# Five edits to a four-layer graph network kernel: zeros of the adjacency, entries of two layers, alternating PSUM banks in the edge loop

## The chip, the cores and the metric

The kernel is one program on one core of a Trainium2 chip. The metric is the device time of one execution in microseconds (us); lower is better. The program's queues are PE (matmul), ACT, DVE (vector), POOL (GpSimd) and SP, which only issues transfers.

## The reference

A graph of 3125 nodes with 64 features each and 103,125 edges (50,000 random pairs in both directions and a self loop for each node), sorted by destination; each edge has one of 16 types. Four layers run one after the other, each as `x = x + layer(relu(layernorm(x)))`:

- L0: two SAGE convolutions (`segment_sum(x[src], dst) @ Wl.T + bl + x @ Wr.T`) with a row normalisation between them.
- L1: relational sums; an edge of type r adds `h[src] @ weight[r]` to its destination.
- L2: three GAT attention convolutions, each with self loops added: `softmax` over the incoming edges of `leaky_relu(h[src] @ a_src + h[dst] @ a_dst)`, weighting `h[src]`.
- L3: two mean SAGE convolutions with batch norm and leaky ReLU.

## The kernel before

**Layout.** Nodes lie as 25 tiles (NT) of 125 partitions (P), so features are `[125, 25, 64]`; five chunks (NC) of five tiles (TC) are the unit of the pipelines. The adjacency `adj` holds the number of edges between each pair of nodes in FP16, 25 tiles of 125 x 3146 (39,325 FP32 words on each partition). It must be zero before it is built, and it serves L0, L2 and L3.

**Preparation (L165 to L258).** SP loads the edge tables, then features and matrices (L170 to L176); after the index work on DVE it stores `key_table` (L178). POOL fills the first half of `adj` with zeros (L188), ACT the second (L200), while DVE waits for nothing but its tables and runs a chain of index operations (L217 to L258). The block ends when all engines have, SP's waits for every load among them. Then comes a loop that builds `adj` by one-hot matmuls (L364).

**L1's entry (L398 to L719).** Before L1 the last five tiles of `adj` are stored in DRAM (`adj_saved`), since L1 uses their space for its buffers. A block does LayerNorm over all 25 tiles, `x_saved` is stored (L398), a second block splits the normalised features into FP16 high and low parts (`h_parts`, L644 to L653) and stores them as `h_table` in DRAM (L658, L659), and a third loads the relation weights (L695, L696, scaled at L703), makes an index row by a POOL `iota` (L708, cast at L719) and zeroes the sums `aggT`.

**L1's edge loop (L738 to L1030).** 34 turns (TURNS), each with six groups (`pos` 0 to 5) of 512 edges. Of these, POOL fetches four (`pos` 0, 1, 3, 4: buffers 0 to 3) with four indirect gathers each (L761) from `h_table`; each gather buffer is free again once PE's `z` of that position in the turn before is done. The other two (`pos` 2 and 5) are picked by PE: DVE makes 25 one-hot `select` rows of 1024 edges (L951, five buffers), and PE multiplies `h_parts` with them (`pick`, L896, two matmuls each) into PSUM banks 3 and 4. At the turn's end ACT copies banks 3 and 4 to `picked_T` (L812), PE turns the eight blocks (`turned`, L906) into banks 5 and 6, and ACT copies these to `pair_pick` (L817), which the next turn's `z` 2 and 5 read. `z` (L875) multiplies gathered rows with one-hots of destination and type (DVE L939, ACT L794 and L800), ACT copies `z` out of PSUM (L824), and `outputs` (L885) applies the 16 relation weights, in six parts over the next turn. DVE adds the 20-column windows to `aggT` (L963). PE's order in a turn is written out by hand:

```python
z(j, pos)
if pos == 0 and not static(j, 0):
    turned(j)
if not static(j, LAST):
    pick(j, lo, hi)
if not static(j, 0):
    outputs(j - 1, 1 - half, *PARTS[pos])
```

After the loop two turns' windows are added, each with its base loaded just before (`base_of`), the barriers pass and SP clears 23 semaphores.

**L2's entry (L1244 to L1342).** SP reloads `x_saved`, the vectors and the five tail tiles of `adj` (L1250 to L1253), each as one transfer of 125 rows; DVE waits for the features, adds L1's sums by chunk (L1270), does LayerNorm over all tiles (L1275 to L1285) and the attention vectors' columns of three layers (L1294, L1295); PE turns and projects chunk by chunk (L1579, L1587). POOL adds self loops to the first 20 tiles (L1473), sets constants (L1476, L1480), adds the self loops of the tail tiles as they land (L1485), and takes the maximum over partitions (L1488), on which DVE's next steps wait (L1316, then L1342). PE counts degrees (L1562) once all self loops are in. L2's first columns follow at L1342 on DVE.

Of the kernel before, what the change touches and what calls it, by code (L numbers as in the profile page):

```python
# [38 lines left out]
PICKED = {2: 0, 5: 1}  # L39
TAIL = 20  # L40
# [30 lines left out]
def gnn(nc, x_in, dst_groups, src_groups, src_tiles, dst_tiles, type_tiles, mats_in, vecs_in, rel_in, out):  # L71
    ctx = ExitStack()
    with ctx:
# [50 lines left out]
        node_key = sb("node_key", [P, NT], FP32, edge_scope)  # L124

# [12 lines left out]
        iota_h = sb("iota_h", [128, W * NT], FP16, build_scope)  # L138
# [20 lines left out]
        zero_cut = adj_words.shape[1] // 2  # L159
# [5 lines left out]
        with block as block:  # L165
            @block.sync
            def _(sp):
# [4 lines left out]
                sp.dma_start(ti[:, 2, :], type_tiles).then_inc(s_ti, 16)  # L172
                sp.dma_start(x_sb[:, :, :], x_in).then_inc(s_x, 16)
# [3 lines left out]
                sp.wait_ge(s_key, 1)  # L177
                sp.dma_start(key_table.rearrange("(k g) e -> g k e", g=128), key_i.bitcast(FP16)).then_inc(s_keys, 16)  # L178
                for s in (s_mats, s_mats2, s_vecs, s_x, s_keys):
                    sp.wait_ge(s, 16)  # L180

            @block.gpsimd
            def _(pool):
# [4 lines left out]
                pool.memset(adj_words[:, 0:zero_cut], 0.0).then_inc(s_zeroed, 1)  # L188
# [83 lines left out]
        with nc.Fori(0, passes):  # L272
            with nc.Block() as block:
                @block.vector
# [304 lines left out]
        with nc.Block() as block:  # L579
            @block.sync  # L580
            def _(sp):
                sp.dma_start(adj_saved, adj_tail).then_inc(s_spill, 16)
                for done in (s_sg, s_key, s_keys, s_nodes, s_dg, s_ti, s_x, s_mats, s_mats2, s_vecs, s_zeroed, s_zeroed2, s_iota,
                             s_ident, s_ident2, s_chain, s_diag, s_basebc, s_span, s_spanall):
                    sp.sem_clear(done)
# [47 lines left out]
        with ExitStack() as scope:  # L633
            h = sb("l1_h", [P, NT, D], FP32, scope)
            tmp = sb("l1_tmp", [P, NT, D], FP32, scope)

            layer_norm_relu("l1", h[:, :, :], tmp[:, :, :], dmas=[(x_saved, x_flat)])
            s_hs, s_table, s_hp, s_lp = (sem("l1_" + n) for n in ("h_scaled", "table_stored", "high_parts", "low_parts"))
            cut = 112
            rows = table.rearrange("(t p) d -> p t d", p=P)  # L640
            with nc.Block() as block:
                @block.vector
                def _(dve):
                    nc.vector.tensor_scalar(tmp[:, :, :], h[:, :, :], LO_SCALE, None, ALU.mult).then_inc(s_hs, 1)  # L644
                    dve.wait_ge(s_hp, 1)
                    dve.wait_ge(s_hs, 1)
                    nc.vector.scalar_tensor_tensor(h_parts[:, :, D:2 * D], h_parts[:, :, 0:D], -LO_SCALE, tmp[:, :, :],
                                                   ALU.mult, ALU.add).then_inc(s_lp, 1)
                    dve.wait_ge(s_lp, 1)

                @block.scalar
                def _(act):
                    act.activation(h_parts[:, :, 0:D], h[:, :, :], ACT.Copy).then_inc(s_hp, 1)  # L653

                @block.sync
                def _(sp):
                    sp.wait_ge(s_lp, 1)
                    sp.dma_start(rows[0:cut], h_parts[0:cut, :, :]).then_inc(s_table, 16)  # L658
                    sp.dma_start(rows[cut:P], h_parts[cut:P, :, :]).then_inc(s_table, 16)  # L659
                    sp.wait_ge(s_table, 32)  # L660
                    sp.wait_ge(s_spill, 16)

# [1074 lines left out]
```

## Time and profile before

| | |
|---|---|
| time, median of 3 | 2373.18 us (2372.23 to 2378.6) |
| the profiled execution | 2376.6 us, its span 2374.8 us |
| PE / DVE / ACT / POOL busy | 75% / 70% / 52% / 47% of the span |
| mean granted TensorE clock | 0.89 |
| preparation | 0 to 35.5 us |
| building `adj` | 35.5 to 375 us |
| L0 | 376.5 to 487.2 us |
| L1's entry | 487.7 to 516.5 us |
| L1's edge loop, its closing barriers with it | 516.5 to 1437.1 us |
| L2's entry, up to DVE L1342 | 1437.1 to 1489.4 us |
| L2 and L3 | to 2374.8 us |

The stages follow one another: a barrier stands between them. So what a stage saves at its end is saved in the whole, and what an engine saves inside a stage only counts if the stage's end moves. The profiled execution took 3.4 us more than the median, 0.14%.

### The profile page before, as it was taken

The numbers are of one execution on the slowest core, as the hardware profiler recorded it, in microseconds if no ns is written. First come the engines' busy times: TensorE is split into PE (matmuls) and PEld (weight loads), VectorE is DVE, ScalarE is ACT, GpSimd is POOL, SyncE is SP. The second block draws the span as 40 slices with busy tenths as digits, with TensorE's granted clock in tenths as the row PEclk, the third lists the DMA queues.
The fourth block names the chain that finished last, engine by engine and source line by source line (L and its number), as shares of the span: only waits on it lengthen the run. The fifth ranks groups of instructions, "written<-read, shape, count | busy, mean of one in ns | idle before, by whom it ended". The sixth has DMA issues, their size and how long they took to land. (4 is left out here: it accounts for less than half of the span.)

```text
span 2374.8 us, 34792 instructions
## 1 busy us (share of the span) xinstructions
PE 1783.5 (75%) x8596; PEld 861.0 (36%) x8597; DVE 1667.6 (70%) x4201; ACT 1237.7 (52%) x2384; POOL 1124.7 (47%) x1008
## 2 busy tenths in 40 slices
PE   2777776825788878887888784678967896788676
PEld 0222223512344444443444444324332333233344
DVE  9999994353566655665666553899779977998554
ACT  5777773122333333333333330489948994799411
POOL 3000000026666666666666651368836884688500
PEclk9999998967888988898889885799979997999877
DMA  1000001011111111111111112000000000000000
GB/s 64 0 0 0 0 0 67 1 51 27 35 29 28 29 33 29 29 29 32 29 29 30 32 17 100 2 1 1 0 1 1 1 0 1 1 1 0 14 1 14
DMA packets 28833, 44.91 MB, mean 19 GB/s; under 512 B 12401, under 2 KB 13407, under 8 KB 28635
## 3 DMA queue, kind: packets, MB, share of 16 engines
q0 software_dynamic: 17664, 18.12, 4.4%
q1 hardware_dynamic: 11096, 25.89, 2.9%
q8 instruction: 36, 0.59, 0.1%
q14 instruction: 37, 0.30, 0.0%
HBM read 36.58 MB, written 7.39 MB: 19 GB/s over the span
## 5 line engine op out<-in xcount | busy, mean ns | idle before, releaser
L761 POOL DMA_INDIRECT adj<-h_table,l_idx x544 | 563.1, 1035 | 321.8 <-issue 149.5
L951 DVE TENSOR_SCALAR adj<-adj,node_key 125x1024 f16<-125x1024 f16 x825 | 379.5, 502 | 361.7 <-remote 154.3
L1495 POOL TENSOR_TENSOR gat_ring<-gat_ring,adj 125x750 f32<-125x750 f32 (+2 forms) x375 | 502.8, 1341 | 214.8 <-ACT gat_ring L1551 211.2
L896 PE MATMUL psum<-adj,x_sb 125*128 125x512 f16 x1650 | 445.9, 418 | 34.6 <-DVE adj L951 28.7
L824 ACT ACTIVATE l_z<-psum 128x320 f32<-128x320 f32 x204 | 89.3, 438 | 567.2 <-remote 225.1
L1389 DVE SCALAR_TENSOR_TENSOR gat_ring<-x_sb,gat_node,psum 125x750 f32<-125x750 f32 (+2 forms) x375 | 318.8, 858 | 52.4 <-PE psum L1627 41.7
L1549 ACT ACTIVATE gat_ring<-gat_ring,gat_node 125x750 f32<-125x750 f32 (+2 forms) x375 | 304.2, 811 | 63.2 <-DVE gat_ring L1389 59.6
L1624 PE MATMUL psum<-gat_ring,gat_hx 125*65 125x500 f32 (+1 forms) x500 | 257.3, 608 | 67.8 <-POOL gat_ring L1495 67.1
L364 PE MATMUL psum<-col_hot,src_hot 128*128 128x500 bf16 x808 | 206.1, 377 | 97.1 <-DVE src_hot L293 76.5
L1551 ACT ACTIVATE gat_ring<-gat_ring 125x750 f32<-125x750 f32 (+2 forms) x375 | 271.8, 725 | 11.9
L1358 DVE SCALAR_TENSOR_TENSOR psum<-adj,gat_node,psum 125x750 f32<-125x750 f16 (+1 forms) x276 | 257.0, 931 | 1.3
L896 PEld LDWEIGHTS psum<-adj,x_sb 125*128 125x128 f16 x1650 | 171.0, 106 | 235.5 <-issue 63.4
L290 DVE TENSOR_SCALAR col_hot<-iota_h,c_tab 128x500 bf16<-128x500 f16 x808 | 227.4, 345 | 25.5 <-PE psum L364 21.5
L708 POOL IOTA l_z<- 128x320 int32 x1 | 0.4, 393 | 488.2 <-issue 488.2
L875 PE MATMUL psum<-adj 128*128 128x320 bf16 x816 | 150.7, 308 | 46.6 <-DMA adj<-h_table,l_idx 43.5
L545 PE MATMUL psum<-adj,l_parts 125*128 125x500 f16 x1000 | 146.2, 308 | 47.9 <-DVE l_parts L494 47.9
L330 ACT ACTIVATE adj<-psum 125x500 f32 x202 | 123.0, 609 | 79.5 <-PE psum L368 73.4
L885 PE MATMUL psum<-l_z,l_rel 128*64 128x120 f32 x1088 | 163.2, 287 | 0.0
L1624 PE MATMUL psum<-gat_ring,gat_o 125*65 125x500 f32 (+1 forms) x250 | 127.1, 601 | 34.3 <-POOL gat_ring L1495 33.9
L939 DVE TENSOR_SCALAR adj<-l_iota,adj 128x320 bf16<-128x320 f16 x612 | 149.4, 298 | 2.3 <-PE psum L875 1.8
L885 PEld LDWEIGHTS psum<-l_z,l_rel 128*64 128x64 f32 x1088 | 116.3, 144 | 92.3 <-issue 92.1
L364 PEld LDWEIGHTS psum<-col_hot,src_hot 128*128 128x128 bf16 x808 | 65.8, 97 | 222.9 <-DVE src_hot L293 170.0
(243 smaller groups left out, 2037.9 us busy)
## 6 DMA issues: line engine op xcount, KB each, us to landing
adj<-h_table,l_idx POOLq DMA_INDIRECT x544
adj<-key_table SPq DMA_DIRECT2D x33, 250.0 KB
adj_saved<-adj SPq DMA_DIRECT2D x1, 3840.3 KB
adj<-adj_saved SPq DMA_DIRECT2D x5, 768.1 KB
x_saved<-x_sb SPq DMA_DIRECT2D x2, 781.2 KB
x_sb<-x_saved SPq DMA_DIRECT2D x2, 781.2 KB
x_sb<-in_x SPq DMA_DIRECT2D x1, 781.2 KB
out<-x_sb SPq DMA_DIRECT2D x5, 156.2 KB
```

The costliest lines, as they stand in the source:

```text
L290: last = v.tensor_scalar(col_hot[:, at, t, :], iota_h[:, :], c_tab[:, bass.ds(g * GT + t, 1)], None, ALU.is_equal)
L364: last = pe.matmul(sums, src_hot[:, at, t, :], col_hot[:, at, t, :], start=(t == 0), stop=False)
L761: pool.indirect_dma_start(out=to[:, t, :], out_offset=None, in_=table[:, :], in_offset=bass.IndirectOffsetOnAxis(ap=index[:, t:t + 1], axi ...
L885: last = pe.matmul(psum[0:D, SUMS[half], 0:SIX * W], rel[:, r, :], zs[:, half, r, :, :].rearrange("p a w -> p (a w)"), start=(r == 0), sto ...
L896: last = pe.matmul(psum[:, 3 + t, :], h_parts[:, k, :], select[0:P, k % SELECTS, t * GE:(t + 1) * GE], start=(k == 0), stop=(k == NT - 1), ...
L951: v.tensor_scalar(select[0:P, k % SELECTS, :], keys, node_key[:, k:k + 1], None, ALU.is_equal).then_inc(s_sel, 1)
L1358: v.scalar_tensor_tensor(to, here, a_unit[:, k:k + 1], so_far, ALU.min, ALU.max).then_inc(s["max_step"], 1)
L1389: v.scalar_tensor_tensor(by_tile(ring[:, n % RING, 0:width(c)]), by_tile(rrow[:, 0:width(c)]), k_s[:, k:k + 1], in_psum(ROW1, c), ALU.add, ...
L1495: pool.tensor_tensor(slot, slot, adj[:, k, cols(c)], ALU.mult).then_inc(s["weight_ready"], 1)
L1549: act.activation(slot, slot, ACT.Relu, scale=-1.0, bias=neg_a_s[:, k:k + 1]).then_inc(s["exponent_bounded"], 1)
L1551: act.activation(slot, slot, ACT.Exp, scale=-1.0).then_inc(s["exp_ready"], 1)
L1624: last = pe.matmul(sums[:, 0:near, 0:P], hx[:, k, :], by_tile(ring[:, n % RING, 0:near * P]), start=(k == 0), stop=(k == NT - 1))
```

## The change

1. Zeros: POOL fills 3800 words of `adj` only; SP copies them three times, each in parts of 112 and 13 partitions; ACT zeroes from word 15,200 on. The loads of features, matrices and vectors go behind the copies and the `key_table` store on SP's queue, and are waited for in the build loop.
2. L1's entry is one block: LayerNorm and the split are done by chunk, ACT makes the scaled copy too, each chunk is stored when it is ready; the `iota` and its cast are gone (`iota_h` is kept for the edge loop), POOL zeroes all of `aggT`.
3. The edge loop: picks of turns with `half` 0 go to banks 3 and 4, those with `half` 1 to banks 5 and 6, and `turned` writes into the pair from which ACT has just copied the picks of the turn before. In PE's turn, `turned` follows the first picks and the first part of `outputs`. After the picks, SP loads the features again (`x_kept`).
4. After the loop: the bases of a turn's six windows are loaded before the first of them is added; four engines share the clearing of semaphores.
5. L2's entry: no reload of the features; sums added and reduced by chunk, squares on ACT, the columns of layer 1 ahead of the wait for the square root and the rest behind the chunks, PE waits for the first layer's only; transfers split in 112 and 13 rows; tail tiles in the order 22, 23, 24, 20, 21.

```diff
-        zero_cut = adj_words.shape[1] // 2
+        pool_words, copies = 3800, 3
+        act_from = (copies + 1) * pool_words
+                sp.wait_ge(s_zeroed, 1)
+                for k in range(1, copies + 1):
+                    for rows in even:
+                        sp.dma_start(adj_words[rows, k * pool_words:(k + 1) * pool_words], adj_words[rows, 0:pool_words])\
+                            .then_inc(s_zero_dma, 16)
+                sp.wait_ge(s_key, 1)
+                sp.dma_start(key_table.rearrange("(k g) e -> g k e", g=128), key_i.bitcast(FP16)).then_inc(s_keys, 16)
                 sp.dma_start(x_sb[:, :, :], x_in).then_inc(s_x, 16)
...
-                pool.memset(adj_words[:, 0:zero_cut], 0.0).then_inc(s_zeroed, 1)
+                pool.memset(adj_words[:, 0:pool_words], 0.0).then_inc(s_zeroed, 1)
...
-                act.memzero(adj_words[:, zero_cut:]).then_inc(s_zeroed2, 1)
+                act.memzero(adj_words[:, act_from:]).then_inc(s_zeroed2, 1)
...
-                pool.iota(ri, pattern=[[1, RW]], base=0, channel_multiplier=0).then_inc(s_iw, 1)
-                pool.memset(aggT[:, 2 * (AW // 3):], 0.0).then_inc(s_pz, 1)
+                pool.memset(aggT[:, :], 0.0).then_inc(s_pz, 1)
...
+                for c, tiles in enumerate(chunks):
+                    sp.wait_ge(s_lp, c + 1)
+                    sp.dma_start(rows[0:cut, tiles, :], h_parts[0:cut, tiles, :]).then_inc(s_table, 16)
+                    sp.dma_start(rows[cut:P, tiles, :], h_parts[cut:P, tiles, :]).then_inc(s_table, 16)
+                act.wait_ge(s_rel, 32)
+                act.activation(rel[D:2 * D, :, :], rel[D:2 * D, :, :], ACT.Copy, scale=1.0 / LO_SCALE).then_inc(s_relc, 1)
+                act.wait_ge(s_moved, 16)
+                for c, tiles in enumerate(chunks):
+                    act.wait_ge(s_norm, c + 1)
+                    act.activation(h_parts[:, tiles, 0:D], h[:, tiles, :], ACT.Copy).then_inc(s_hp, 1)
+                    act.activation(tmp[:, tiles, :], h[:, tiles, :], ACT.Copy, scale=LO_SCALE).then_inc(s_hs, 1)
...
+        PAIR = (3, 5)
+                    sp.wait_ge(s_selmm, NT * LAST)
+                    sp.dma_start(x_kept[0:EVEN], x_saved[0:EVEN]).then_inc(s_x_back, 16)
+                    sp.dma_start(x_kept[EVEN:P], x_saved[EVEN:P]).then_inc(s_x_back, 16)
...
-                            act.activation(picked_T[:, k, :], psum[:, 3 + k, :], ACT.Copy).then_inc(s_pT, 1)
+                            act.activation(picked_T[:, k, :], psum[:, PAIR[1 - half] + k, :], ACT.Copy).then_inc(s_pT, 1)
...
-                                last = pe.matmul(psum[:, 3 + t, :], h_parts[:, k, :],
+                                last = pe.matmul(psum[:, PAIR[half] + t, :], h_parts[:, k, :],
...
-                                last = pe.matmul(psum[:, 5 + k, edge], picked_T[:, k, edge], ident16[:, :],
+                                last = pe.matmul(psum[:, PAIR[1 - half] + k, edge], picked_T[:, k, edge], ident16[:, :],
...
                             z(j, pos)
-                            if pos == 0 and not static(j, 0):
-                                turned(j)
                             if not static(j, LAST):
-                                pick(j, lo, hi)
+                                pick(j, half, lo, hi)
                             if not static(j, 0):
                                 outputs(j - 1, 1 - half, *PARTS[pos])
+                                if pos == 0:
+                                    turned(j, half)
...
+                        bases = [base_of(j, pos) for pos in range(SIX)]
                         for pos in range(SIX):
-                            add_window(j, pos, base_of(j, pos), half)
+                            add_window(j, pos, bases[pos], half)
...
-            sp.dma_start(x_flat, b["x_saved"]).then_inc(s["x_back"], 16)
...
+    tail_order = [*range(TAIL + KEPT_TILES, NT), *range(TAIL, TAIL + KEPT_TILES)]
+            def tail(t):
+                for rows in row_parts:
+                    sp.dma_start(adj[rows, t, :], b["adj_saved"][rows, (t - TAIL) * AW:(t - TAIL + 1) * AW]).then_inc(s_tail[t], 16)
...
-                link(v.tensor_tensor(h_in, tmp, tmp, ALU.mult))
-                link(v.tensor_reduce(stat[:, 1, :], h_in, AX.X, ALU.add))
+                for c, tiles in enumerate(chunks):
+                    dve.wait_ge(s["ln_squared"], c + 1)
+                    link(v.tensor_reduce(stat[:, 1, tiles], h_in[:, tiles, :], AX.X, ALU.add))
                 v.tensor_scalar(stat[:, 1, :], stat[:, 1, :], 1.0 / D, LN_EPS, ALU.mult, ALU.add).then_inc(s["ln_var"], 1)
+                weight_columns(0)
...
-            pe.wait_ge(s["w_columns"], 2 * LAYERS)
+            pe.wait_ge(s["w_columns"], 2)
```

## Rows read from the trace of the kernel before

**Rows 1.** Groups by line, 573.5 to 1414.7 us: busy us, mean ns, idle before by releaser
```profile
L761 POOL DMA_INDIRECT adj<-h_table,l_idx x514 | 532.6, 1036 | 307.2 <-issue 141.0 <-PE psum L875 101.6 <-remote 64.6
```

**Rows 2.** The instructions of one line, L812: durations, first and last start
```profile
L812 ACT ACTIVATE l_picked_T<-psum x66: 587/594/599, 573.5 to 1414.7; 128x512 f16<-128x512 f32 x66
```

**Rows 3.** Waits, 573.5 to 1414.7 us: us in total, times, longest us
```profile
PE psum L906 <- ACT l_picked_T L812: 123.4, 30, 5.1
```

**Rows 4.** Windows: length, busy of PE, PEld, DVE, ACT, POOL (count), clock, DMA share, GB/s
```profile
571.00:1440.00 869.00, 715.57 (x3760) 366.36 (x3758) 512.91 (x1600) 310.68 (x756) 536.91 (x525) 0.89 0.14 29
...
994.00:1000.50 6.50, 5.56 (x22) 2.90 (x22) 4.06 (x14) 3.93 (x10) 3.96 (x4) 0.50 0.11 20
...
1440.00:1480.00 40.00, 19.12 (x90) 17.72 (x90) 18.07 (x41) 4.27 (x8) 8.07 (x23) 0.50 0.32 130
```

**Rows 5.** Timeline, 985 to 1003 us: start, us, engine, line, [idle before <-releaser]
```profile
989.55 0.72 PE L875 MATMUL psum<-adj 128*128 128x320 bf16 x4
...
993.69 0.88 DVE L951 TENSOR_SCALAR adj<-adj,node_key 125x1024 f16<-125x1024 f16 x2 [3.32 <-remote]
...
994.60 1.00 POOL L761 DMA_INDIRECT adj<-h_table,l_idx  x1 [2.17 <-remote]
...
994.94 1.09 PE L906 MATMUL psum<-ident,l_picked_T 128*128 128x128 f16 x8 [4.67 <-ACT l_picked_T L812]
...
995.83 3.62 PE L896 MATMUL psum<-adj,x_sb 125*128 125x512 f16 x8
...
1000.68 0.72 PE L875 MATMUL psum<-adj 128*128 128x320 bf16 x4
...
1001.23 1.89 PE L896 MATMUL psum<-adj,x_sb 125*128 125x512 f16 x8
...
1002.18 0.99 POOL L761 DMA_INDIRECT adj<-h_table,l_idx  x1 [2.70 <-PE psum L875]
```

**Rows 6.** Timeline, 2 to 36 us, and the DMA view's GB/s, 40 slices of 0 to 35 us
```profile
2.02 16.59 ACT L200 ACTIVATE adj<-adj 125x19663 uint32<-125x19663 uint32 x1
...
2.21 16.58 DVE L217 TENSOR_SCALAR iota_neg<-iota_h 128x128 f16<-128x128 f16 x1
2.26 16.48 POOL L188 MEMSET adj<- 125x19662 f32 x1
...
18.82 0.69 DVE L220 CAST dg_i<-dg_i 128x1024 f32<-128x1024 int32 x1
...
35.49 0.69 ACT L316 ACTIVATE square<-iota_h,lo_tab 128x128 f16<-128x128 f16 x2 [16.88 <-PEq L165]
...
GB/s 0 0 136 323 412 410 403 418 414 401 132 102 124 139 139 124 135 115 85 1 0 0 0 0 0 0 0 0 0 0 191 109 0 0 0 0 0 0 0 0
```

**Rows 7.** Timeline, L1's entry, 487 to 518 us
```profile
497.52 1.54 ACT L653 ACTIVATE x_sb<-l_h 125x1600 f16<-125x1600 f32 x1 [2.70 <-PEq L391]
...
514.60 1.00 DVE L719 CAST l_iota<-l_z 128x320 f16<-128x320 int32 x1 [6.84 <-POOL l_z L708]
```

**Rows 8.** Timeline, end of the edge loop and L2's entry, 1424 to 1490 us
```profile
1426.24 0.17 DVE L963 TENSOR_TENSOR l_aggT<-l_aggT,psum 64x20 f32 x1 [0.58 <-DVE l_aggT L963]
...
1437.30 2.35 PE L1571 MATMUL psum<-ident,l_aggT 64*125 64x64 f32 x10 [8.48 <-PEq L1037]
...
1446.45 0.89 DVE L1270 TENSOR_TENSOR x_sb<-x_sb,psum 125x320 f32<-125x320 f32 x2 [12.41 <-DMA x_sb<-x_saved]
...
1454.89 1.83 DVE L1278 TENSOR_TENSOR gat_o<-gat_ring 125x1600 f32<-125x1600 f32 x1
...
1479.58 0.18 DVE L1311 TENSOR_REDUCE gat_ext<-gat_scores 125x1 f32<-125x25 f32 x1
...
1481.41 0.42 POOL L1485 TENSOR_TENSOR adj<-adj,ident 125x125 f16<-125x125 f16 x1 [5.51 <-DMA adj<-adj_saved]
...
1487.80 0.37 POOL L1488 PARTITION_ALL_REDUCE gat_ext<-gat_ext  x1 [5.97 <-issue]
...
1489.40 1.12 DVE L1342 TENSOR_SCALAR psum<-adj,gat_node 125x375 f32<-125x375 f16 x2
```

More of the change, by code:

```diff
@@ L39 @@
 PICKED = {2: 0, 5: 1}
+EVEN = 112
 TAIL = 20
@@ L176, in _ @@
                 sp.dma_start(vecs0[:, :, :], vecs_in[:, 0:2 * D].to_broadcast([P, 2 * D])).then_inc(s_vecs, 16)
[L177 to L180, printed above, removed]
+                sp.wait_ge(s_zero_dma, 32 * copies)
+                sp.wait_ge(s_keys, 16)
             @block.gpsimd
@@ L273, in gnn, with _ @@
             with nc.Block() as block:
+                @block.sync
+                def _(sp):
+                    for loaded in (s_mats, s_mats2, s_vecs, s_x):
+                        sp.wait_ge(loaded, 16)
                 @block.vector
@@ L632, in gnn @@
         table = nc.dram_tensor("h_table", [N, 2 * D], FP16, kind="Internal").ap()
[L633 to L661, printed above, removed]
         l1_scope = ExitStack()
@@ L687, in gnn @@
         pair_pick = carve(2 * GT * 2 * D).rearrange("p (k t d) -> p k t d", k=2, t=GT)
-        ri = zs[:, 0, 0:4, :, :].rearrange("p r a w -> p (r a w)").bitcast(I32)[:, 0:RW]
-        rf = sb("l1_iota", [128, RW], FP16, l1_scope)
-        s_iw, s_ic, s_rel, s_relc, s_az, s_pz = (sem("l1_" + n) for n in (
-            "iota", "init_chain", "weights_in", "weights_scaled", "zeroed_by_act", "zeroed_by_pool"))
+        rf = iota_h[:, 0:RW]
+        s_moved, s_centred, s_squared, s_var, s_std, s_lc, s_norm, s_hp, s_hs, s_lp, s_table = (sem("l1_" + n) for n in (
+            "x_saved", "ln_centred", "ln_squared", "ln_var", "ln_std", "ln_chain", "normalised", "high_parts", "h_scaled",
+            "low_parts", "table_stored"))
+        s_rel, s_relc, s_pz = (sem("l1_" + n) for n in ("weights_in", "weights_scaled", "zeroed_by_pool"))
+        rows = table.rearrange("(t p) d -> p t d", p=P)
+        features = free[0:P, 0:4 * NT * D].bitcast(FP32).rearrange("p (k t d) -> p k t d", k=2, d=D)
+        h, tmp = features[:, 0, :, :], features[:, 1, :, :]
+        chunks = [slice(c * TC, (c + 1) * TC) for c in range(NC)]
+        cut = 112
         with nc.Block() as block:
@@ L727, in gnn @@
         s_key = sem("l1_keys_in", l1_scope)
+        s_x_back = sem("l1_features_back", l1_scope)
+        x_kept = free[0:P, 0:2 * NT * D].bitcast(FP32)
         ENG = mybir.EngineType
@@ L889, in outputs, with pick @@
                             last.then_inc(s_sum, 1)
-                    def pick(j, lo, hi):
+                    def pick(j, half, lo, hi):
                         for k in range(lo, hi):
@@ L899, in pick, with turned @@
                             last.then_inc(s_selmm, 1)
-                    def turned(j):
+                    def turned(j, half):
                         for k in range(2):
@@ L1201, in attention @@
     assert all(len(d) - DEG_EARLY <= GC - 1 for d in deg_tiles)
-    names = ("x_back", "agg_transposed", "x_added", "vecs_in", "x_kept", "ln_chain", "ln_var", "ln_std", "ln_chunk",
+    row_parts = (slice(0, EVEN), slice(EVEN, P))
+    KEPT_TILES = -(-2 * NT * D // AW)
+    tail_order = [*range(TAIL + KEPT_TILES, NT), *range(TAIL, TAIL + KEPT_TILES)]
+    x_kept = b["x_kept"]
+    chunks = [slice(c * TC, (c + 1) * TC) for c in range(NC)]
+    names = ("agg_transposed", "x_added", "vecs_in", "x_kept", "ln_chain", "ln_centred", "ln_squared", "ln_var", "ln_std", "ln_chunk",
              "self_loops", "w_chain", "w_columns", "w_rows", "constants", "transposed", "transpose_copied", "first_projected",
@@ L1264, in add_aggregate @@
             def add_aggregate():
-                dve.wait_ge(s["x_back"], 16)
-                for c in range(NC):
+                link = Chain(dve, s["ln_chain"])
+                for c, tiles in enumerate(chunks):
                     dve.wait_ge(s["agg_transposed"], c + 1)
-                    tiles = slice(c * TC, (c + 1) * TC)
                     part = psum[0:P, c % 2, 0:TC * D].rearrange("p (t d) -> p t d", d=D)
-                    v.tensor_tensor(x_sb[:, tiles, :], x_sb[:, tiles, :], part, ALU.add).then_inc(s["x_added"], 1)
```

151 lines of the change are left out of this document (100 added, 51 removed).

## The prediction

> **What bounds the kernel now.** I read the page for the stages first, then for each stage what its end waits for. The edge loop is the largest, 869 of 2375 us, with PE busy for 716 of them and POOL for 537 [rows 4]. Neither share names the bound, so I read the loop by turns. The copy L812 comes in pairs, 66 in all, first at 573.5 and last at 1414.7: 32 turns in 841.2 us, 26.3 each [rows 2]. In that stretch POOL issues 514 gathers in 532.6 us (16.6 a turn), has 141.0 us of "issue" between them (4.4 a turn), and waits 101.6 + 64.6 = 166.2 us (5.2 a turn) for a `z` of PE that frees a buffer [rows 1]. The three make the turn: POOL is always gathering or waiting for PE. So 21.0 us a turn is POOL's own floor, and 166.2 us is the most that a better order of PE can give.
>
> PE in its turn waits 123.4 us, in 30 waits, for ACT's `picked_T` before it can turn the picked rows [rows 3]. One turn shows how that costs [rows 5]. PE's last `z` starts at 989.55; DVE gets on only at 993.69 and POOL at 994.60; PE turns at 994.94; the picks behind it run at the lower TensorE clock, 0.50 in this stretch, which is 1.2 GHz [rows 4], so that eight take 3.62 us instead of 1.89; the second `z` starts at 1000.68, and POOL, which needs it, has waited 2.70 us at 1002.18 [rows 5].
>
> **The change, part by part.**
>
> *Zeros.* DVE's L217, 128 columns, is shown for 16.58 us and ends with POOL's memset; only then does the index chain begin, at 18.82, and the stage ends 16.7 us later [rows 6]. POOL fills 0.838 ns a word, so 3800 words take 3.2 us, to about 5.5; the chain then gives a stage end of 22.2. ACT's share grows to 24,125 words at 0.844 ns, 20.4 us: its end at 22.4, with 1.1 for the barrier 23.5. The copies are 3 x 3800 words x 125 rows = 5.7 MB. Loads reach 412 GB/s [rows 6]; behind some 2.2 MB of tables (until about 7.7) they take 13.8 us, to 21.5, and `key_table`, now behind them on SP's queue, 2 us more: with the barrier 24.6, against 35.5. That is -11. Features and matrices come later, under the 340 us of the build loop, which hides them; uncovered they would cost some 3 us. No row shows a copy inside SBUF: at the full rate ACT binds, -12; at half the rate the copies end at 35.3 and the stage at 38.4, +3. I take the full rate, as the nearest row is of transfers on 16 engines. Were it ACT's fill (ended 18.61) and not POOL's that held DVE, the chain would end at 39, +3.6.
>
> *L1's entry.* Before, ACT copies `h_parts` at 497.52 after a barrier, the stores land near 506.4, and then DVE's cast is held 6.84 us by POOL's iota; the loop begins 0.9 us after the cast, at 516.5 [rows 7]. After, the third block's work lies beside the first: no barrier (-1), but ACT does the scaling of the relation weights (1.05) and two copies of 1.54 a piece in chunks, so the last store issues near 502.5 and lands near 506, and the loop starts at 506.9: -9.6. If the weights, behind `x_saved` on the queue, are late by 3 us it is -6; if the stores overlap better, -12. POOL's start after the iota was late because of a code load; if a cast at the loop's beginning takes that load over, 7 of the 9.6 come back: -2.6.
>
> *Edge loop.* Selects 2 and 3 still need the last picks of the turn before, so the release at 993.69 stays. They are ready at 994.57. Then PE does picks 2 and 3 (half of 3.62: 1.81), the outputs (1000.68 less the picks' end, 1.23), `turned` (1.09), and the second `z` starts at 998.7 rather than 1000.68: -2.0; with the picks at the higher clock (0.95) -2.9 [rows 5]. POOL can use only what it waits there, 101.6 us in 58 waits, 1.75 at a time [rows 1]. I take 1.9 us a turn, -60. The lower bound is nothing (the release at 993.69 might move later by what the rest gains), the upper -166. The new load of `x_kept` goes after the last pick and has over 20 us of windows and outputs ahead of the barrier; uncovered it would cost about 8.
>
> *After the loop.* The windows' bases stand in the way for 0.58 us each [rows 8]; loaded in two groups of six, I count -2.2, and -1.0 for the split clears: -3, between 0 and -7 (12 x 0.58).
>
> *L2's entry.* DVE waited 12.41 us for the features, until 1446.45; now it can add when PE's first five transposes are done, near 1439, since ten take 2.35 us from 1437.30 [rows 8]: -7.4. From there to L1311 (33.1 us before) the square (1.83) goes to ACT, the sums go along with the additions, and PE no longer waits for six columns: -3.5 together. Then 9.8 us pass before L1342, because POOL's maximum L1488 starts 6 us after POOL is free, while it should follow L1311 at once; the tail tiles came one by one until 1481.41. With them in by 1453 and POOL ready early, 2.5 remain: -7.3. Sum -18.2, with 13 us of degree counting on PE still covered. Less if POOL loads code ahead of L1473 instead: the constants behind it come 6 us later and the projection waits for them, -12; at best -20.
>
> The tail tiles' share can be read from the DMA column. While transfers of 125 rows run it stands at 0.32 and 130 GB/s, under a third of the 412 seen in loading [rows 4, 6]; split in 112 and 13, each tile of 0.77 MB should take about 2 us, not 5.9. The Trainium skill ("DMA: Bandwidth & Descriptors", section "Why a DMA increments its semaphore by 16 and not by 1") says that a transfer uses the largest number of engines up to 16 that divides its slowest dimension: 5 for 125 rows, 16 for 112. By that rule the trace agrees, 0.32 being 5 of 16.
>
> The same skill speaks against the gain on POOL: "GPSIMD Engine Reference" says that the first call to a freshly loaded kernel pays about 6 us. The trace agrees, 5.97 before L1488; by that rule the load is moved, not removed, and the sum is as in the third rival.
>
> **The sum.** -11 - 9.6 - 60 - 3 - 18.2 = -102 against the profiled execution's 2376.6 us (its span 2374.8 and 1.8 around it); against the median of 2373.2 that is 2271. Without the loop the edits outside give -42.
>
> **The rivals.**
> - The loop gains nothing: the release from PE to DVE and POOL comes 4 us after PE's recorded end [rows 5], and if it follows POOL's gathers and not PE's order, the wait only moves. For it: DVE, ACT and POOL are released together. 2373 - 42 = 2331.
> - The boundary goes altogether: with no wait PE stays at the higher clock and POOL runs near its floor, 21.6 us a turn. 4.7 x 32 = 150: 2181. Against it: selects 2 and 3 and the outputs still stand behind the same release.
> - POOL's code loads move to where they are waited for: +7 in L1's entry and +6 in L2's: 2284.
> - Copies inside SBUF run at half rate, or DVE is held by ACT: +14: 2285.
> - Slower: `turned` comes 3 us later, so `pair_pick` may be late for `z` 2, at which PE stands each turn, and POOL's next buffers with it. It decides from 1.3 us a turn (42 / 32); at 2 us a turn 2373 - 42 + 64 = 2395. Against it: `turned` ends near 998.7 and ACT's copy 1.2 later, near 1000, while `z` 2 is due near 1002.
>
> **How the numbers follow.** The forecast, 1 to 3 us a turn (with either of the small rivals in it), 2235 to 2300: 0.50. The loop gains under 1 us a turn: 0.24. Over 3: 0.15. It loses up to 1.2 us a turn, the whole still faster: 0.05. Slower beyond 0.3%: 0.04; within 0.3%, 7 us, which is what a measurement can tell from no change: 0.02. The range runs from 2190, inside the second rival, to 2342, the first one with 11 lost on zeros; some 0.08 is left below and 0.1 above. Faster 0.94, same 0.02, slower 0.04.
>
> **What the profile after would show.** The build loop starting near 24.6; L1's entry 19 us long (was 29); turns of 24.4 us, PE's wait for L812 gone and POOL's waits for `z` down to about 100; L2's entry 34 us long with no gap of 6 ahead of L1488. The prediction is wrong if turns stay at 26 or fall under 23, if PE stands at `z` 2 for L817, or if copies inside SBUF pass 20 us.

## The result, and the profile after

The changed kernel took 2342.12 us (2337.44 to 2345.74, 4 runs) against 2372.97 us for the kernel before (2372.23 to 2378.6, 4 runs): a ratio of 0.9859, 95% interval 0.9839 to 0.9878. So it is faster, by 31 us, where 102 were forecast; 2342.12 lies 0.12 us outside the range. The profiled execution took 2340.22 us, with a span of 2338.4; that is 36.4 us under the profiled execution of before, since the latter was 3.6 us above its median and this one 1.9 below.

Stage by stage, each from the first instruction of one stage to the first of the next (us), the two profiles differ like this:

| stage | before | after | forecast |
|---|---|---|---|
| preparation | 35.6 | 35.6 | -11 |
| building `adj`; L0 | 342.7; 109.4 | 342.0; 111.0 | 0 |
| L1's entry | 28.8 | 19.1 | -9.6 |
| edge loop to the first L812/L851 | 57.0 | 57.0 | 0 |
| 32 turns | 841.2 | 828.5 | -60 |
| last turns and closing | 22.6 | 20.0 | -3 |
| L2's entry | 52.1 | 40.4 | -18.2 |
| the rest | 885.4 | 884.8 | 0 |

Preparation, the changed kernel's timeline:

```profile
2.21 3.36 DVE L226 TENSOR_SCALAR iota_neg<-iota_h 128x128 f16<-128x128 f16 x1
2.26 3.26 POOL L197 MEMSET adj<- 125x3800 f32 x1
...
5.55 11.26 SPq L180 DMA_DIRECT2D adj<-adj  x6
5.61 0.69 DVE L229 CAST dg_i<-dg_i 128x1024 f32<-128x1024 int32 x1
...
21.07 0.15 DVE L267 TENSOR_SCALAR npass<-gstat 128x1 int32<-128x1 f32 x1
...
35.50 0.69 ACT L330 ACTIVATE square<-iota_h,lo_tab 128x128 f16<-128x128 f16 x2 [13.17 <-PEq L169]
```

and its DMA view, 40 slices of 0 to 38 us, and the time of one transfer from issue to landing:

```profile
GB/s 0 30 116 379 413 405 409 402 524 288 256 256 272 288 256 224 128 112 256 256 352 240 320 304 144 160 256 240 240 272 219 308 207 92 173 233 153 135 135 135
...
key_table<-sg_i SPq DMA_DIRECT2D x1, 256.0 KB, 17.6
```

DVE is let go with POOL's memset, as worked out, and is done at 21.2. But where the loads moved 412 GB/s, many slices under the copies show 256 and some 112 to 224, and `key_table`, behind them in the queue, lands at 34.5. The stage ends where it ended before [rows 6], now on SP.

L1's entry, its last part:

```profile
498.86 1.05 ACT L702 ACTIVATE l_rel<-l_rel 64x1024 f32<-64x1024 f32 x1 [2.30 <-DMA l_rel<-in_rel]
...
505.48 0.50 SPq L691 DMA_DIRECT2D h_table<-x_sb  x1
...
507.68 0.20 POOL L813 CAST l_idx<-src_tab 128x16 uint32<-128x16 int16 x1 [16.40 <-POOLq L682]
```

The 6.84 us behind the iota [rows 7] are gone, and ACT waits 2.3 for the weights instead.

The edge loop, 564.7 to 1393.2 us (32 turns of 25.9): the instructions of the line that was L812, then groups, then waits:

```profile
L851 ACT ACTIVATE l_picked_T<-psum x66: 587/594/599, 564.7 to 1393.2; 128x512 f16<-128x512 f32 x66
```

```profile
L800 POOL DMA_INDIRECT adj<-h_table,l_idx x512 | 524.5, 1024 | 304.8 <-issue 139.3 <-remote 89.0 <-PE psum L914 76.6
```

```profile
ACT l_z L863 <- remote: 222.9, 44, 7.8
...
PE psum L935 <- DVE adj L990: 131.8, 65, 5.4
```

PE's 123.4 us of waiting for ACT [rows 3] are gone, and 131.8 us of waiting for DVE's selects stand in their place. POOL waited 166.2 us for PE [rows 1]; now 89.0 + 76.6 = 165.6 ("remote" stands where a signal came but the profile finds no instruction that gave it at that time). One turn of the timeline, to set beside [rows 5]:

```profile
978.38 0.88 DVE L990 TENSOR_SCALAR adj<-adj,node_key 125x1024 f16<-125x1024 f16 x2 [4.56 <-remote]
...
982.53 1.03 PE L945 MATMUL psum<-ident,l_picked_T 128*128 128x128 f16 x8
...
983.36 1.27 PE L914 MATMUL psum<-adj 128*128 128x320 bf16 x4
...
985.86 1.15 POOL L800 DMA_INDIRECT adj<-h_table,l_idx  x1 [1.58 <-PE psum L914]
...
997.44 0.72 PE L914 MATMUL psum<-adj 128*128 128x320 bf16 x4
...
1004.19 0.44 ACT L863 ACTIVATE l_z<-psum 128x320 f32<-128x320 f32 x1 [7.78 <-remote]
...
1005.18 1.00 POOL L800 DMA_INDIRECT adj<-h_table,l_idx  x1 [2.42 <-remote]
```

The last `z` of the turn starts at 997.44 and is over at 998.2; ACT, with nothing else to do, copies it at 1004.19. The release at the turn's boundary is as late as it was [rows 5]: POOL gathers again at 1005.18, having waited 2.42 us where it waited 2.17. These 6 to 7 us between the end of a `z` in PE's records and the engines that wait for it are called the late release below.

L2's entry, and the configuration records of L1534 (the line that was L1473):

```profile
1414.59 0.49 DVE L1329 TENSOR_TENSOR x_sb<-adj,psum 125x320 f32<-125x320 f32 x1 [4.09 <-PE psum L1635]
...
1424.00 0.41 POOL L1534 TENSOR_TENSOR adj<-adj,ident 125x125 f32 x1 [10.83 <-issue]
1424.72 9.38 POOL L1534 TENSOR_TENSOR adj<-adj,ident 125x125 f32 x19 [0.31 <-issue]
...
1434.29 1.13 POOL L1541 MEMSET gat_hT<- 1x1250 f32 x1
...
1436.15 1.22 PE L1643 MATMUL psum<-ident,gat_o 125*64 125x125 f32 x5 [7.98 <-POOL gat_weights L1541]
...
1452.00 0.37 POOL L1549 PARTITION_ALL_REDUCE gat_ext<-gat_ext  x1 [14.13 <-DVE gat_ext L1375]
...
1453.61 1.12 DVE L1402 TENSOR_SCALAR psum<-adj,gat_node 125x375 f32<-125x375 f16 x2
```

```profile
L1534 POOLq MODIFY_POOL_CONFIG  x40: 1/8/11, 1413.3 to 1433.6; - x40
```

The features and the partition maximum no longer hold anybody up, but POOL's self loops start 10.8 us into the stage, behind a configuration record (`MODIFY_POOL_CONFIG`) at 1413.3, and PE stands 8 us for the constants behind them.

### The profile page after: what moved, and what is told of

It is laid out like the page before. It is cut to its first block and busy times, and to the rows that moved or that the text cites. A ratio compares the mean times of both kernels' runs of the same rounds, so it can differ in the third digit from the quotient of the medians.

```text
span 2338.4 us, 34869 instructions
## 1 busy us (share of the span) xinstructions
PE 1768.6 (76%) x8596; PEld 852.4 (36%) x8597; DVE 1648.2 (70%) x4217; ACT 1248.4 (53%) x2397; POOL 1107.6 (47%) x1007
## 5 line engine op out<-in xcount | busy, mean ns | idle before, releaser
L800 POOL DMA_INDIRECT adj<-h_table,l_idx x544 | 556.7, 1023 | 320.2 <-issue 148.4
L990 DVE TENSOR_SCALAR adj<-adj,node_key 125x1024 f16<-125x1024 f16 x825 | 372.4, 494 | 358.6 <-remote 170.3
L935 PE MATMUL psum<-adj,x_sb 125*128 125x512 f16 x1650 | 436.2, 405 | 158.2 <-DVE adj L990 150.6
L935 PEld LDWEIGHTS psum<-adj,x_sb 125*128 125x128 f16 x1650 | 160.5, 102 | 367.0 <-DVE adj L990 193.9
L914 PE MATMUL psum<-adj 128*128 128x320 bf16 x816 | 155.6, 316 | 40.1 <-DMA adj<-h_table,l_idx 32.5
L978 DVE TENSOR_SCALAR adj<-iota_h,adj 128x320 bf16<-128x320 f16 x612 | 149.2, 298 | 0.5 <-issue 0.3
```

Of the source, the lines that this page charges most:

```text
L800: pool.indirect_dma_start(out=to[:, t, :], out_offset=None, in_=table[:, :], in_offset=bass.IndirectOffsetOnAxis(ap=index[:, t:t + 1], axi ...
L935: last = pe.matmul(psum[:, PAIR[half] + t, :], h_parts[:, k, :], select[0:P, k % SELECTS, t * GE:(t + 1) * GE], start=(k == 0), stop=(k == ...
L990: v.tensor_scalar(select[0:P, k % SELECTS, :], keys, node_key[:, k:k + 1], None, ALU.is_equal).then_inc(s_sel, 1)
```

## The experiments

The chips that these kernels met differ, and only in the edge loop. A is the chip of the result, B to E those of the experiments:

| chip | kernel | time, us (executions) | us a turn |
|---|---|---|---|
| A | before | 2372.97 (4) | 26.3 |
| A | changed | 2342.12 (4) | 25.9 |
| B | before | 2354.03 (9) | no trace |
| B | old order of PE | 2331.24 (5) | 25.6 |
| B | no copies | 2313.74 (1) | 25.2 |
| B | ACT held back | 2340.26 (1) | 25.3 |
| B | early code load | 2316.64 (4) | 25.4 |
| C | before | 2217.54 (7) | no trace |
| C | changed | 2201.15 (4) | 21.8 |
| C | no key loads | 2205.31 (1) | 21.8 |
| C | SP loads for gathers | 2099.81 (1) | 19.3 |
| C | mended | 2184.79 (4) | 21.8 |
| D | before | 2344.76 and 2347.01 | 25.5 |
| D | no key loads | 2322.40 (1) | 25.1 |
| D | SP loads for gathers | 2098.51 (1) | 19.3 |
| D | half the gathers | 2105.84 (1) | 19.4 |
| E | before | 2217.14 (7) | no trace |
| E | changed | 2198.12 (4) | 21.7 |
| E | old order of PE | 2196.85 (4) | 21.6 |
| E | pauses between gathers | 2319.19 (1) | 25.2 |
| E | mended | 2185.70 (4) | 21.8 |

Every stage that a kernel left untouched outside the loop was within 3 us of the table above on all of them. So a kernel is compared only with others of its own chip. Each chip was met once; that the chip makes the difference, and not something else that held for all the executions there, is not shown.

**What the copies cost.** Two edits of the preparation on chip B.

```diff
-        pool_words, copies = 3800, 3
+        pool_words, copies = 3800, 0
...
-                sp.wait_ge(s_zero_dma, 32 * copies)
```

> The changed kernel without the copies inside SBUF: POOL fills 3800 words, ACT zeroes all the others (35,525). If the copies set the end of the preparation (35.5 us in the changed kernel), it now ends with ACT: 35,525 words at 0.842 ns from 2.0 is 31.9, with the barrier 33.0. If something else held the block, such as the index chain or the key table, it stays at 35.5. The key table then lands within 3 us of its issue instead of 17.6.

```diff
+                act.wait_ge(s_zero_dma, 32 * copies)
                 act.memzero(adj_words[:, act_from:]).then_inc(s_zeroed2, 1)
```

> The changed kernel with ACT's zeros held back until all copies have landed, so that the copies run with no engine writing zeros beside them. Theory 1 (a copy inside SBUF moves at about half the rate of a load, whatever the engines do): the copies land near 33 as before, ACT fills from 33 to 53.5, the preparation ends near 55. Theory 2 (ACT's writes slow the copies): they land near 22, the preparation ends near 43.

Without the copies (timeline, DMA view):

```profile
2.03 29.81 ACT L208 ACTIVATE adj<-adj 125x35525 uint32<-125x35525 uint32 x1
...
32.87 0.69 ACT L329 ACTIVATE square<-iota_h,lo_tab 128x128 f16<-128x128 f16 x2 [1.03 <-PEq L169]
```

```profile
key_table<-sg_i SPq DMA_DIRECT2D x1, 256.0 KB, 2.2
```

With ACT held back (timeline):

```profile
33.57 20.31 ACT L210 ACTIVATE adj<-adj 125x24125 uint32<-125x24125 uint32 x1 [31.55 <-DMA adj<-adj]
```

Without copies the preparation is 33.0 us, as expected, and the key table lands in 2.2 us, not 17.6: the copies set the end. With ACT idle they land at 33.5 and the key table behind them at 34.1; in the twelve kernels with ACT's fill beside the same copies the key table lands at 33.7 to 36.8. So the fill doesn't explain the rate, though that it costs up to 3 us isn't excluded. From about 7.7 to 33.5 the 5.7 MB have moved at 220 GB/s on average. Left out altogether the copies are better than three of them: 33.0 us against 37.5 and 38.0 for two kernels with them on the same chip.

**The code load.** On chip B, one instruction more for POOL in L1's entry:

```diff
                 pool.memset(aggT[:, :], 0.0).then_inc(s_pz, 1)
-                pool.wait_ge(s_pz, 1)
+                pool.iota(zs[:, 0, 0:4, :, :]...bitcast(I32)[:, 0:RW], pattern=[[1, RW]], base=0,
+                          channel_multiplier=0).then_inc(s_pz, 1)
+                pool.wait_ge(s_pz, 2)
```

> The changed kernel with one more POOL iota (128 x 320, nobody reads it) in L1's entry, behind the memset of the sums, where POOL idles for 16 us. Theory 1 (the first such POOL instruction after the partition reduce pays a code load, and the gathers of the edge loop leave the code in place): the load of 6 to 8 us lies hidden in L1's entry, the self loops of L2's entry start at once instead of 10.9 us late, and the first L2 columns on DVE start 6 to 8 us earlier after the loop: about 2335. Theory 2 (the edge loop's gathers or casts put other code in its place, so L2's entry pays in any case): no change, 2342.

Its timeline in L1's and L2's entry (the self loops, L1534 in the changed kernel, are L1536 here):

```profile
500.65 0.39 POOL L713 IOTA l_z<- 128x320 int32 x1 [6.95 <-issue]
```

```profile
1397.34 7.46 POOL L1536 TENSOR_TENSOR adj<-adj,ident 125x125 f32 x20
...
1430.24 1.12 DVE L1404 TENSOR_SCALAR psum<-adj,gat_node 125x375 f32<-125x375 f16 x2
```

The ratio to the kernel before is 0.9839 (0.9815 to 0.9862). L2's entry is 33.0 us instead of 40.4, and the self loops start at once and take 7.46 us instead of 10.1. The load now lies in L1's entry, where POOL idles 6.95 us for it and nobody waits. So the first theory holds, and casts and gathers in between leave the code in place. The time of 2316.64 is under the 2335 expected because chip B is faster in the loop.

**The order of PE in the edge loop**, undone: `turned` directly behind the first `z`, picks always in banks 3 and 4, as in the diff ahead, read backwards.

> The changed kernel with the edge loop's edit undone: picks always in banks 3 and 4, turned right behind the first z, everything else as changed. Theory 1 (the new order of PE is worth what the two profiles show, 12.7 us over 32 turns, and the release at the turn's boundary sets the rest): about 2355, turns of 26.3 us, PE waiting about 123 us for ACT's picked rows again. Theory 2 (the order is worth nothing, the 12.7 us are scatter between executions): about 2342, turns of 25.9. If the new order were worth the 60 us of the prediction and something else in the changed kernel cost 47, this would be near 2400.

> Once more the changed kernel with the edge loop's edit undone, now beside the changed kernel on the same chip. On a chip with the late release the new order is worth 8 to 15 us (the first time 10 by the ratios, across two calls); on one without it, where POOL's floor sets the turn, nothing: within 4 us of the changed kernel.

> The changed kernel itself, on the same chip as the three beside it, as their reference: 0.986 of the kernel before, give or take 0.002.

> The changed kernel as the reference of this call: 0.986 of the kernel before on a chip with the late release, 0.993 on one without.

> The kernel before itself, for its trace on this chip beside the others. The chips differ in the edge loop alone: the kernel before took 2373, 2354 and 2218 us on the chips so far. If it comes out near 2218, turns are 21.8 us or so at POOL's floor and PE's signals reach the others at once; if near 2360, turns are near 26 and the release at the turn's boundary comes 4 to 6 us after PE.

On chip B the old order has 0.9903 (0.9886 to 0.9919) of the kernel before, turns of 25.6 us; with the new order the three other kernels there had turns of 25.2, 25.3 and 25.4. By the medians the kernel with the early code load is 14.6 us below the old order, of which L2's entry gives 7.4, so that 7 remain for the order. On chip E old and new order ran side by side: 0.9909 (0.9892 to 0.9926) and 0.9915 (0.9898 to 0.9931), turns of 21.6 and 21.7 us. The changed kernel on chip C: 0.993 (0.991 to 0.9949), turns of 21.8, where 0.986 was expected. So the new order is worth some 0.2 to 0.5 us a turn on a chip like A or B, and nothing on E. The first is near the scatter: four executions of one kernel on chip B lay 10 us apart, which is 0.3 a turn. The groups show why. Old order on chip B, old and new on chip E, kernel before on chip D, each over its 32 turns:

```profile
L800 POOL DMA_INDIRECT adj<-h_table,l_idx x513 | 532.3, 1038 | 285.0 <-issue 142.7 <-PE psum L914 78.9 <-remote 63.5
```

```profile
L800 POOL DMA_INDIRECT adj<-h_table,l_idx x515 | 535.3, 1039 | 156.9 <-issue 148.7 <-PE psum L914 8.2
```

```profile
L800 POOL DMA_INDIRECT adj<-h_table,l_idx x515 | 538.9, 1046 | 156.9 <-issue 149.3 <-PE psum L914 7.6
```

```profile
L761 POOL DMA_INDIRECT adj<-h_table,l_idx x514 | 532.8, 1036 | 284.9 <-issue 141.6 <-PE psum L875 75.7 <-remote 67.6
```

A gather takes nearly the same on all chips, 1.02 to 1.05 us. On C and E POOL waits 7 to 8 us in 32 turns for PE and goes at its floor of 21.6 to 21.8 us a turn; on A, B and D it waits 131 to 166. That is where the chips differ: from A to C the changed kernel has 158 us less of these waits, of which longer gathers and pauses between them take back 28. Over the 32 turns of the changed kernel on chip C the clock is 0.97, with PE busy for 640 of 697 us (windows); on A it was 0.92:

```profile
545.50:1242.70 697.20, 640.03 (x3648) 337.49 (x3648) 503.58 (x1562) 307.98 (x736) 540.57 (x515) 0.97 0.18 35
```

**Who makes the release late.** Three theories: K, the key load that SP issues just before a turn ends; P, PE itself behind its records; G, POOL's gathers. The kernels for them leave out keys or indices, so that L1's sums are wrong in them.

```diff
-                    with sp.Fori(1, TURNS // 2 - 1) as q:
-                        for half in range(2):
-                            sp.wait_ge(s_sel, NT * (2 * q - 1 + half) + 1)
-                            keys(2 * q + half, half)
...
-                        if not static(j, LAST):
+                        if static(j, 0) or static(j, 1):
                             dve.wait_ge(s_key, 16 * (j + 1))
```

> The changed kernel in which SP loads the keys of the first two turns only and all later turns select by these (this leaves out 31 of the 33 key loads, so L1's picked edges are wrong). It asks whether the key load that SP issues shortly before each turn's end delays the release of ACT, DVE and POOL by PE. Theory K (it does): turns fall from 25.2 to 25.9 us to about 22, POOL's waits for PE from 5.2 us a turn to under 2. Theory G (the release is late because of POOL's gathers) and theory P (PE itself runs behind its records): turns stay at 25 to 26.

> Once more the changed kernel that loads keys for the first two turns only (it leaves out 31 key loads, L1's picked edges are wrong), since the first time it met a chip without the late release, where it changed nothing (turns of 21.8 us with and without). Theory K on a chip with the late release: turns fall to about 22. Theories G and P: they stay above 25.

```diff
+                    def load(to, done):
+                        for t in range(GT):
+                            sp.dma_start(to[:, t, :], table[t * ET:(t + 1) * ET, :]).then_inc(done, 16)
+                    def fetch(j):
+                        for k in range(4):
+                            sp.wait_ge(s_z, SIX * (j - 1) + FREED[k])
+                            load(got[:, k, :, :], s_got[k])
...
-                    with nc.Fori(1, TURNS // 2, engines=[ENG.Pool], head_slot={ENG.Pool: 0}) as q:
-                        fetch(2 * q, 0)
-                        fetch(2 * q + 1, 1)
```

> The changed kernel with POOL's 544 gathers replaced by SP's plain loads of the same size and places (128 fixed rows of 256 bytes each; this leaves out the indices, so L1's sums are wrong); POOL idles in the edge loop. Theory G (what PE signals reaches ACT, DVE and POOL late while POOL issues gathers back to back): the copy of the last z of a turn follows PE within 1 us instead of 4 to 6, no boundary wait is left, and the turn is PE's own work, 21 us or less, so the loop is 130 to 200 us shorter. Theory P (PE runs behind its records, whoever loads): the late release stays, turns of 24 us or more.

> Once more the changed kernel with all gathers replaced by SP's plain loads of fixed rows (it leaves out the indices, L1's sums are wrong). On the chip without the late release turns were 19.3 us with the clock at 1.00. Theory G on a chip with it: the same 19 to 20 us, since no gather delays a signal, clock near 1.00. Theory P: turns above 22.

Half of each, with `range(GT // 2)` on POOL and `range(GT // 2, GT)` on SP:

> The changed kernel with half of POOL's gathers (the second two of each four) replaced by SP's plain loads of fixed rows, which leaves out their indices, so L1's sums are wrong. Theory G (signals of PE come late while POOL issues gathers back to back): on a chip with the late release the wait of ACT for the last z falls from 4 to 6 us to 2 or less and turns from 25 to 26 us to 19 to 21; on a chip without it, turns fall from 21.8, POOL's floor, to PE's 19.4. Theory P (PE runs late by itself on such a chip): turns stay above 23 there.

The first of each pair met chip C, where nothing is late, so it only gives the floors: 21.8 us a turn without key loads, 19.3 without gathers. The second met chip D, beside the kernel before with turns of 25.5. Windows of the 32 turns there, without key loads, without gathers, with half of them:

```profile
567.70:1371.90 804.20, 677.78 (x3650) 335.24 (x3649) 503.68 (x1565) 306.43 (x736) 526.26 (x511) 0.94 0.11 21
```

```profile
530.60:1149.70 619.10, 617.70 (x3649) 331.35 (x3648) 485.78 (x1565) 304.83 (x737) 0.00 (x0) 1.00 0.16 40
```

```profile
536.50:1157.40 620.90, 618.88 (x3641) 332.10 (x3642) 491.31 (x1562) 308.30 (x736) 273.91 (x256) 1.00 0.17 40
```

Without key loads the turn stays at 25.1 us: K falls. Without gathers it is 19.3 us, the same as on chip C (2098.5 and 2099.8 us in all): P falls, since PE does the same work with no delay. With half the gathers it is 19.4, PE busy for 99.7% of it and the clock at 1.00, which is 2.4 GHz; ACT's waits for `z` are the same with half of them and with none, 240.1 and 239.2 us in 32 turns. The late release needs POOL's gathers in a dense row, on some chips. SP's loads differ from the gathers in their kind of transfer as well as in who issues them, so which of the two counts isn't shown.

The first turns of the same traces bear G out without any edit. There POOL has free buffers and gathers on without a wait. In the kernel before on chip A (timeline):

```profile
547.57 1.27 PE L875 MATMUL psum<-adj 128*128 128x320 bf16 x4
...
564.48 0.94 POOL L761 DMA_INDIRECT adj<-h_table,l_idx  x1 [0.30 <-issue]
569.77 0.44 ACT L824 ACTIVATE l_z<-psum 128x320 f32<-128x320 f32 x1 [24.77 <-remote]
```

That `z` is over at 548.8 in PE's records, and ACT, idle for 24.8 us, copies it at 569.8, 4.4 us after POOL's last gather has ended. In the kernel before on chip D the same `z` is copied 20.3 us after its end and 3.6 after POOL's last gather; in the changed kernel on A 17.2 and 4.6. On chip C, where the gathers lie as densely, the copy starts at once. From the loop's start to the first copy of `picked_T` it is 56 to 60 us for the kernels with all gathers on A, B and D, 38 to 40 for those on C and E (42 with the pauses asked for next), and on chip D 30.3 with half the gathers and 24.8 with none.

Whether a pause between them is enough was asked in another way:

```diff
                             ).then_inc(done, 16)
+                            for _ in range(12):
+                                pool.sem_inc(s_tick, 1)
```

> The changed kernel with twelve increments of a semaphore that nobody waits for behind each of POOL's gathers, so that some 0.5 us lie between two gathers beside the 0.3 that lie there now. POOL's floor rises from 21 to about 29 us a turn. Theory G in the form that back-to-back issue delays PE's signals: on a chip with the late release the delay shrinks (ACT's wait for the last z in the turn counted from PE's end falls under 2 us), and turns are near the new floor, 29 to 30. If each gather delays what comes after it whatever lies between: turns near 33 to 34, floor and late release added up.

It met chip E, so it says nothing of the late release. 32 turns took 807.6 us instead of 694.2, 25.2 a turn where 29 was expected: the time between gathers rose by 92 us (0.18 for each of the 512 and not 0.5), POOL's waits for PE by 39, and the gathers took 22 less. What the pause does where the release is late is open.

**A mended version**: fewer words to copy and one copy of them, and the early code load.

```diff
-        pool_words, copies = 3800, 3
+        pool_words, copies = 6500, 1
...
+                pool.iota(zs[:, 0, 0:4, :, :]...bitcast(I32)[:, 0:RW], pattern=[[1, RW]], base=0,
+                          channel_multiplier=0).then_inc(s_pz, 1)
```

> The changed kernel with POOL filling 6500 words, one copy of these by SP, ACT zeroing 26,325 words, and the additional POOL iota in L1's entry. Theory (from the two preceding runs: a copy inside SBUF moves about 250 GB/s, the code load hides in L1's entry): preparation 25 to 26 us instead of 35.6, L2's entry 33 us instead of 40.4, so 17 us less than the changed kernel on the same chip. Rival: the copies again end last, preparation over 30, gain under 12.

> Once more POOL 6500 words, one copy, ACT 26,325 words, and the early POOL iota, now beside the changed kernel and on whichever chip: 15 to 17 us under the changed kernel (8 from the preparation, 7.5 from L2's entry), since neither edit touches the edge loop.

The preparation on chip E (timeline):

```profile
2.02 22.15 ACT L209 ACTIVATE adj<-adj 125x26325 uint32<-125x26325 uint32 x1
...
14.71 0.42 SPq L183 DMA_DIRECT2D key_table<-sg_i  x1
...
27.03 0.69 ACT L330 ACTIVATE square<-iota_h,lo_tab 128x128 f16<-128x128 f16 x2 [2.86 <-PEq L169]
```

On chip C 2184.79 us, 0.9851 (0.9835 to 0.9868) of the kernel before, where the changed kernel has 2201.15; on chip E 2185.70, 0.986 (0.9843 to 0.9876), where it has 2198.12. That is 16 and 12 us less than the changed kernel, where 17 and 15 to 17 were expected. The preparation is 27.1 to 27.4 us and not 25 to 26 (the single copy still holds the key table up until 26), L2's entry 32.7 to 33.1. It wasn't run on a chip with the late release.

## Why the prediction was wrong

**Edge loop: the step that failed.** "I take 1.9 us a turn, -60" was mis-sized, and the reason stood in its own bound: that the release might move later by what the rest gains. What the step said of PE came true to the tenth: from DVE's release to the second `z` it was 7.0 us (993.69 to 1000.68) and is 5.0 (978.38 to 983.36). POOL, which next needs that `z`, got 1.0 of the 2.0 in this turn: 8.5 us after DVE's release (1002.18) before, 7.5 after (985.86). Over the turns with their 16 gathers complete in the trace (over 20 in each) its idle time ahead of that fifth gather fell from about 1.9 to 1.2 us, ahead of the ninth it rose from 1.5 to nearly 1.7, ahead of the thirteenth from 0.3 to 0.6 or 0.7, and at the boundary it stayed, 2.2 and 2.3. So POOL's waits for PE came to 165.6 us instead of 166.2, part of them now booked as "remote" (89.0 instead of 64.6). The turn kept 0.4 us, 12.7 in all, and 8 of these are gathers that took less (524.5 instead of 532.6 us, two fewer of them in the stretch). That is the first rival, nearly in full. It had a chance of 0.24; the row that spoke for it, that ACT, DVE and POOL are let go together and long after PE's record, should have weighed more than a sum over one turn. The experiments on chip D show that the lateness comes with the dense gathers and not from PE's order, its speed or the key loads; that it is the same on A is read from A's own traces, where the first turns look alike. By what path a gather delays a signal isn't settled.

That POOL has a floor of some 21 us a turn was right: 21.6 to 21.8 is what sets the turn on chips C and E. Two of the signs that the prediction named for being wrong came: turns near 26 (25.9), and copies of over 20 us (26). The second rival, a loop at that floor, describes these chips, but there the old order of PE is at the floor as well (turns of 21.6 us on E).

**Zeros: -11 forecast, 0 measured.** DVE's start at 5.6 and ACT's end were right. The rate of a copy inside SBUF was taken from the loads, 412 GB/s; it was 220 on average, so that the 13.8 us became 26. This is the half-rate bound, put at +3 and measured at 0.

**L1's entry: right in size, in part by luck**, -9.6 and -9.7: the weights held ACT for 2.3 us and the last store was issued 2.6 us later in the stage than worked out, but the loop began under 2 us behind it, where over 4 had been counted. **After the loop: -3 forecast, 2.6 in the table, 1.9 shown.** The six windows of a turn now follow each other without a wait, though DVE waits 3.72 us between the two groups: from the first window to L2's first instruction on PE it was 11.8 us, the same on chips A and D, and is 9.9. The rest moves with the last turns, by which the stage of the kernel before is 22.6 us long on A and 20.4 on D.

**L2's entry: -18.2 forecast, -11.7 measured** (on chip D 50.3 us before and 41 to 42 with the change, 8 to 9 less). The features (first addition 1.3 us after PE's first transposes) and the partition maximum (0.3 us after the start of DVE's L1375; before, 7.8 after that of L1313, the same step) came as worked out. What failed is "POOL ready early": with the iota gone from L1's entry, the code load moved ahead of the self loops, the -12 named as the lower end. It was priced near (6.2 us; the kernel with the early code load gives back 7.4, and its 33.0 us are what the forecast had, 34) and given too little weight. Removing an instruction that happened to load the code uncovered the load at the next one. The Trainium skill ("GPSIMD Engine Reference", section "Instruction dispatch") says that the first call to freshly loaded code pays about 6 us. The trace agrees roughly: POOL idles 6.95 us ahead of the iota that hides the load, and 10.83 us ahead of the self loops where nothing hides it. The tail tiles came 3.2 to 3.4 us apart, the last 2.3, in the kernel with the early code load, where 2 were forecast and 5.9 measured before.

**The range.** The three misses have separate causes, and three of the rivals came true in one run, the code loads in their half of L2's entry: 13 + 0 + 9.7 + 2.6 + 11.7 = 37, the spans' 36.4. The range treated the two small ones as alternatives within 14 us of the forecast, not as additions to the first rival; 2331 with 14 and 6 on top is 2351, beyond its end. That the measured time lies only 0.12 us outside is no sign of a sum nearly right: of the 102 us, the loop's 60 came to 13 and the zeros' 11 to nothing.

## What to carry to other kernels

When engines are let go by a signal that comes long after the recorded work, a better order ahead of that signal may only move the wait, as here; ask first what makes the signal late. Removing an instruction from GpSimd can uncover a code load (POOL idled 6 to 11 us in the places seen here) at the next one of its kind: look for the configuration record, and put a cheap instruction of that kind where the engine idles. A transfer in place of an engine's fill should be priced by its own kind of transfer and put on a queue where nothing urgent stands behind it.

## What the runs showed of the hardware

- One program, the kernel before, takes 2345 to 2373 us on three chips and 2217 on two others. For the changed kernel the difference lies wholly in the loop with dense indirect gathers by GpSimd. A turn takes 25.5 to 26.3 us with the old order of PE on the three, against about 21.7 with either order on the two.
- On the slower three, a signal of PE can reach ACT 15 to 21 us after the matmul's recorded end while GpSimd issues gathers 0.3 us apart, and came 3.6 to 4.6 us after the last of them (first turns of four traces: both kernels on A, the old order on B, the kernel before on D).
- Plain loads of the same size by SP in place of the gathers give 19.3 us a turn on both kinds, and half the gathers 19.4 on the slower kind.
- Copies inside SBUF of 15,200 bytes a row, in parts of 112 and 13 rows, ran at 220 GB/s on average and 256 in many slices, loads from DRAM at 412 in the same stage; without an ACT fill beside them they were no faster than in the fastest executions with it.
- PE's 1600 pick matmuls took 377.6 us where the mean granted clock was 1.00 (chip E, old order) and 417.6 us where it was 0.92 (chip A, changed kernel).
